# Two blocks of the shared up projection ahead of the last tiles' transposition, and the shared down weights in quarters

## The chip, the cores and the metric

The kernel runs on one core of one Trainium2 chip. The metric is the device time of one execution in microseconds (us). The kernel before took 1296.97 us, the median of three runs (1294.72, 1296.97 and 1297.15). A core has five engines that run side by side, each with its own instruction order: TensorE (PE), VectorE (DVE), ScalarE (ACT), GpSimd (POOL) and SyncE (SP, which here only issues transfers). They wait for each other by semaphores.

## The reference, cut to what matters

One transformer block on x of 2 x 1024 tokens with 512 features: attention, then a mixture of experts.

```
x = x + attention(layernorm(x))          # 32 heads, 8 key heads, causal
n = layernorm(x).reshape(2048, 512)
logits = n @ router_w                    # 64 experts
scores = softmax(logits);  idx = top_k(logits + router_bias, 4)
gate   = scores[idx] / sum(scores[idx])
routed = sum over the 4 experts of gate * (silu(n @ wg[e]) * (n @ wu[e])) @ wd[e]
shared = sum over s = 0, 1 of (silu(n @ swg[s]) * (n @ swu[s])) @ swd[s]      # swg: 512 x 512
out = x + routed + shared
```

## The kernel before, in words

Tokens lie in 16 tiles of 128 (`t`), and four tiles make a group (`g`) of 512 tokens. The order of every engine is written out by hand; nothing is scheduled by a planner. After attention comes the part that the change touches:

1. **Output projection and second layer norm.** PE projects a group of four tiles (`project`, L1056). DVE adds the result to `X` (L1372), takes the statistics (L1375, L1379) and writes the normalised rows `xn2` (L1389). PE then transposes them (`turn_tokens`, L1065), ACT copies the transposed tile twice (L811 in fp32, L812 in f16 for `x_hi`), PE multiplies with the router (`logits`, L1073), and DVE forms `x_lo`, what the f16 copy lacks (L1362). PE's order is project group 0, project group 1, turn and logits of group 0, project group 2, turn and logits of group 1, and so on; turn and logits of group 3 (tiles 12 to 15) come last.
2. **Routing, on DVE.** It starts only when the logits of all 16 tiles are there (`logits_done`): maximum (L1415), subtraction (L1416), top eight and their indices (L1419, L1422, L1424), then per chosen expert a one-hot matrix (L1427), its product with the exponentials `ex` (L1429) and a sum (L1430), then sums over the tiles (L1438, L1439). That raises `masks_ready`. PE then runs `ranks` (L1093 to L1096), one more block of the shared projection, and `starts` (L1102); DVE goes on with these to slot numbers (L1450 to L1481), and last to the one-hot matrices of the slot table (L1499, L1502), with additions of the shared result in between (L1495).
3. **The shared experts.** A group of 512 tokens has eight up blocks (`n` or `hc` = 0 to 7), each of 24 matmuls in f16: 2 weights (gate and up) x 4 slices x 3 parts (hi x hi, hi x lo, lo x hi; L1130). ACT takes silu (L829) and copies the up half (L833), POOL multiplies them (`hidden`, L706, raises `hidden_done`), ACT rounds that to f16 (`hidden_high`, L821) and POOL forms the rest (`hidden_low`, L698). Block `n` of PE waits for `hidden_done` of block `n - 2`. After the eight blocks come four down tiles (L1151). `ranks` stands behind block 5, `starts` behind block 6. In the second group the product is DVE's (L1485), so PE's block 10 waits for DVE to be done with its table matrices.
4. **The shared down weights `swd`.** Two transfers of 1 MB each bring them to `w_stage`; POOL scales each half (L689), ACT rounds it to f16 (L815, `swd_high` in the new code), POOL forms what is left (L693). All of that stands ahead of `hidden` in POOL's order and ahead of `ex` and silu in ACT's order. PE and SP wait for it with `swd_lo_ready`.

After this region come 96 pairs of 64-slot tiles for the routed experts, the shared experts for groups 2 and 3, and the output.

Of the kernel before, what the change touches and what calls it, by code (L numbers as in the profile page):

```python
# [8 lines left out]
ACT = mybir.ActivationFunctionType  # L9
ALU = mybir.AluOpType  # L10
AXX = mybir.AxisListType.X

P = 128
BATCH, SEQ, D = 2, 1024, 512
NTOK = BATCH * SEQ
NT = NTOK // P
C = D // P
# [3 lines left out]
BANK = 512  # L21
E, F, TOPK = 64, 128, 4
HID = 1024
HC = HID // P
# [10 lines left out]


EARLY = 2

TABLE_AT = HC + 4

# [9 lines left out]
X_SCALE, W_SCALE = 16.0, 64.0  # L50
# [104 lines left out]
def build_block(nc, x, wq, wk, wv, wo, router_w, router_bias, wg, wu, wd, swg, swu, swd, out):  # L155
    ctx = ExitStack()
    with ctx:
# [72 lines left out]
        def q_part(u, h, part):  # L230
# [11 lines left out]
        x_hi, x_lo = carve_all(flat_xn, 0, *[([P, C, NTOK], F16)] * 2)  # L242
        w_stage, x_turned = carve_all(ring, 0, ([P, 2, C * D], FP32), ([P, 4, C * P], FP32))
# [3 lines left out]
        shared_w, swd_w, tmp, mask, cum = carve_all(  # L247
            att, 0, ([P, 4, 2 * C * D], F16), ([P, 2, HC * D], F16), ([P, NT, E], FP32),
            ([P, NT, E], BF16), ([P, NT, E], BF16))
        shared_w = shared_w.rearrange("p n (s d) -> p n s d", s=2 * C)  # L250
        swd_w = swd_w.rearrange("p n (s d) -> p n s d", s=HC)
# [32 lines left out]
        def bank(k, n=BANK):  # L284
            return PS[:, k * BANK:k * BANK + n]
# [49 lines left out]
        swd_scaled = sem("swd_scaled")  # L335
        swd_hi_ready = sem("swd_hi_ready")
        swd_lo_ready = sem("swd_lo_ready")
        hidden_hi_done = sem("hidden_hi_done")
        hidden_lo_done = sem("hidden_lo_done")
        x1_done = sem("x1_done")  # L340
# [10 lines left out]
        x_lo_ready = sem("x_lo_ready")  # L351
        w_hi_ready = sem("w_hi_ready")
        w_lo_ready = sem("w_lo_ready")
        stage_in = [sem("stage_in0"), sem("stage_in1")]
        logits_done = sem("logits_done")
        consts = sem("consts")
        route = sem("route")
        ex_ready = sem("ex_ready")
# [11 lines left out]
        up_done = sem("up_done")  # L370
        silu_done = sem("silu_done")
        up_copied = sem("up_copied")
        hidden_done = sem("hidden_done")
# [61 lines left out]
        def _(sp):  # L435
# [4 lines left out]
            for r in range(REP):  # L440
                for k in range(2):
                    at = (2 * r + k) * HD
# [118 lines left out]
                load_down(i, JP - 1, codes[JP - 1])  # L561

            sp.wait_ge(experts_in, 16)
            sp.wait_ge(swd_lo_ready, 2)
            sp.wait_ge(table_done, 1)
            load_pairs(0, True)
            with sp.Fori(1, LANE_TILES) as i:
# [9 lines left out]
        def _(pool):  # L577
# [106 lines left out]
            pool.affine_select(out=tile_no[:, LANES:], in_=tile_no[:, LANES:], compare_op=ALU.is_gt, fill=-1.0, base=0,  # L684
                               pattern=[[0, LANES]], channel_multiplier=1).then_inc(consts, 1)

            for k in range(2):
                pool.wait_ge(stage_in[k], 16 * 3)
                pool.tensor_scalar(w_stage[:, k, :], w_stage[:, k, :], W_SCALE, None, ALU.mult).then_inc(swd_scaled, 1)  # L689
            for k in range(2):  # L690
                pool.wait_ge(swd_hi_ready, k + 1)
                part = slice(k * C, (k + 1) * C)
                pool.tensor_tensor(swd_w[:, 1, part, :], w_stage[:, k, :].rearrange("p (c n) -> p c n", c=C),  # L693
                                   swd_w[:, 0, part, :], ALU.subtract).then_inc(swd_lo_ready, 1)

            def hidden_low(n):
                pool.wait_ge(hidden_hi_done, n + 1)
                pool.tensor_tensor(hidden_lo[:, n, :], hidden(n), hidden_hi[:, n, :], ALU.subtract)\  # L698
                    .then_inc(hidden_lo_done, 1)

            for n in range(HC):
                pool.wait_ge(silu_done, n + 1)
                pool.wait_ge(up_copied, n + 1)
                if n >= 2:
                    pool.wait_ge(hidden_lo_done, n - 1)
                pool.tensor_tensor(hidden(n), silu_s[:, n % 2, :], up_s[:, n % 2, :], ALU.mult)\  # L706
                    .then_inc(hidden_done, 1)
                if n:
                    hidden_low(n - 1)
            hidden_low(HC - 1)  # L710

            for k in range(TOPK):
# [34 lines left out]
        def _(act):  # L747
# [48 lines left out]
            for g in range(4):  # L796
# [7 lines left out]
                for t in range(4 * g, 4 * g + 4):  # L804
# [5 lines left out]
                    src = bank(4 + t % 2).rearrange("p (c t) -> p c t", c=C)  # L810
                    act.activation(x_turned[:, t % 4, :, :], src, ACT.Copy).then_inc(xt2_ready, 1)  # L811
                    act.activation(x_hi[:, :, t * P:(t + 1) * P], src, ACT.Copy, scale=X_SCALE).then_inc(x_hi_ready, 1)  # L812
            for k in range(2):
                act.wait_ge(swd_scaled, k + 1)
                act.activation(swd_w[:, 0, k * C:(k + 1) * C, :], w_stage[:, k, :].rearrange("p (c n) -> p c n", c=C),  # L815
                               ACT.Copy).then_inc(swd_hi_ready, 1)
            act.wait_ge(route, 2)
            act.activation(ex[:, :, :], tmp[:, :, :], ACT.Exp).then_inc(ex_ready, 1)
            def hidden_high(n):
                act.wait_ge(hidden_done, n + 1)  # L820
                act.activation(hidden_hi[:, n % HC, :], hidden(n), ACT.Copy).then_inc(hidden_hi_done, 1)  # L821

            def shared_silu(g):
                for n in range(HC * g, HC * (g + 1)):
                    act.wait_ge(up_done, n + 1)

                    if n >= 2:
                        act.wait_ge(hidden_done, n - 1)
                    act.activation(silu_s[:, n % 2, :], bank(2 * (n % 2)), ACT.Silu,  # L829
                                   scale=1 / (X_SCALE * W_SCALE)).then_inc(silu_done, 1)  # L830
                    if g == 0:

                        act.activation(up_s[:, n % 2, :], bank(2 * (n % 2) + 1), ACT.Copy,  # L833
                                       scale=1 / W_SCALE).then_inc(up_copied, 1)
                    if n > HC * g:
                        hidden_high(n - 1)
                hidden_high(HC * (g + 1) - 1)

            for g in range(EARLY):
# [45 lines left out]
        def _(pe):  # L885
# [158 lines left out]
            def project(t):  # L1044

                pe.wait_ge(yt_done, C * (t // QT + 1))
                if t == 0:

                    pe.wait_ge(wo_in, 16 * 8)
                    pe.wait_ge(router_in, 16)  # L1050
                    pe.wait_ge(exp_done, 2 * NS * BATCH * KVH)
                    pe.wait_ge(side_read, SIDE * BATCH * KVH)
                if t >= 4:
                    pe.wait_ge(x1_done, t - 3)
                for c in range(C):
                    mm = pe.matmul(bank(t % 4), YT[:, c, t * P:(t + 1) * P], wo_s[:, c, :],  # L1056
                                   start=(c == 0), stop=(c == C - 1))
                mm.then_inc(wo_done, 1)
# [10 lines left out]
            def logits(t):  # L1069
# [4 lines left out]
                                   start=(c == 0), stop=(c == C - 1))  # L1074
                mm.then_inc(logits_done, 1)

            for g in range(5):
                if g < 4:
                    for t in range(4 * g, 4 * g + 4):
                        project(t)  # L1080
                if g >= 1:
                    for t in range(4 * g - 4, 4 * g):
                        turn_tokens(t)
                    for t in range(4 * g - 4, 4 * g):
                        logits(t)
# [28 lines left out]
                                           start=(k == 0 and t == 0), stop=(k == TOPK - 1 and t == NT - 1))  # L1114
                mm.then_inc(table_done, 1)

            pe.wait_ge(x1_done, NT)
            pe.wait_ge(w_lo_ready, 4)
            def shared(g):
                pe.wait_ge(x_lo_ready, 4 * (g + 1))  # L1120
                for hc in range(HC):
                    n = HC * g + hc
                    if n >= 2:
                        pe.wait_ge(hidden_done, n - 1)
                    s, at = hc // C, (hc % C) * P
                    tokens = slice(g * BANK, (g + 1) * BANK)
                    for k in range(2):
                        for c in range(C):
                            for w, v in ((0, x_hi), (0, x_lo), (1, x_hi)):
                                mm = pe.matmul(bank(2 * (n % 2) + k), shared_w[:, 2 * k + w, C * s + c, at:at + P],  # L1130
                                               v[:, c, tokens], start=(c == 0 and w == 0 and v is x_hi),
                                               stop=(c == C - 1 and w == 1))
                    mm.then_inc(up_done, 1)
                    if g == 0 and hc == RANKS_AT:
                        ranks()
                    if g == 0 and hc == STARTS_AT:
                        starts()
                    if n == TABLE_AT:
                        table()
                if g == 0:  # L1140

                    pe.wait_ge(experts_ready, 1)
                    pe.wait_ge(swd_lo_ready, 2)
                for t in range(4 * g, 4 * g + 4):
                    if t >= 2:
                        pe.wait_ge(shared_added, t - 1)
                    for hc in range(HC):
                        if t == 4 * g:
                            pe.wait_ge(hidden_lo_done, HC * g + hc + 1)
                        for w, v in ((0, hidden_hi), (0, hidden_lo), (1, hidden_hi)):  # L1150
                            mm = pe.matmul(bank(4 + t % 2), v[:, hc, (t % 4) * P:(t % 4 + 1) * P], swd_w[:, w, hc, :],  # L1151
                                           start=(hc == 0 and w == 0 and v is hidden_hi),
                                           stop=(hc == HC - 1 and w == 1))
                    mm.then_inc(down_done, 1)
# [469 lines left out]
```

## Time and profile before

| | before |
|---|---|
| median of 3 runs | 1296.97 us |
| lowest to highest | 1294.72 to 1297.15 us |
| the profiled execution's own time | 1296.95 us |
| its span | 1294.9 us |
| mean granted TensorE clock | 0.976 |
| PE / DVE / ACT / POOL busy | 91 / 58 / 38 / 27% of the span |

The span is the time between the first and the last event of the profiled execution; some 2 us lie around it. Shares of busy time are averages over stages that have different limits, so the stretch that the change touches, from about 600 to 760 us, has to be read by itself. A timeline row gives the start, the time covered, the engine and line, the operation, the tile written and the tile read, the partitions x elements and how many instructions were merged, and in brackets the idle time before it and who ended it.

### The profile page before, as it was taken

How to read it: one execution, taken by the hardware profiler on the slowest of the kernel's cores; microseconds unless marked ns; L12 is line 12 of the kernel's file. 1: busy time of each engine (PE TensorE's matmuls, PEld its weight loads, DVE VectorE, ACT ScalarE, POOL GpSimd, SP SyncE). 2: the span in 40 equal slices, each digit the busy share in tenths (PEclk: the TensorE clock that was granted, in tenths of full speed). 3: DMA queues.
4: the chain of work that ended last, by engine and by line, in shares of the span. 5: the costliest groups of instructions: out<-in, count | busy, mean ns of one | idle time of the engine just before them, and what ended most of it. 6: DMA issues, size and time to landing. Idle time of an engine off the chain costs nothing.

```text
span 1294.9 us, 27720 instructions
## 1 busy us (share of the span) xinstructions
PE 1173.3 (91%) x8853; PEld 538.6 (42%) x8854; DVE 745.4 (58%) x1215; ACT 489.9 (38%) x922; POOL 348.9 (27%) x458
## 2 busy tenths in 40 slices
PE   6989788988998998999789989999999999999898
PEld 3534233333333332356333445555444444543343
DVE  5335798999899995557987212233232322327374
ACT  2111587887788788334320212222222221211010
POOL 1000122222222222101736112322222322217561
PEclk9989799999999999999898999999999999999899
DMA  7333232132132120233000347887887688837552
GB/s 228 101 82 102 41 75 39 38 69 41 37 61 49 37 56 2 83 112 131 1 1 1 115 141 251 257 259 261 274 266 244 199 305 311 260 96 230 164 157 70
DMA packets 85556, 169.96 MB, mean 131 GB/s; under 512 B 14852, under 2 KB 17412, under 8 KB 85508
## 3 DMA queue, kind: packets, MB, share of 16 engines
q1 hardware_dynamic: 55764, 100.60, 26.2%
q0 software_dynamic: 12800, 41.95, 11.6%
q10 hardware_dynamic: 16944, 26.75, 6.0%
q8 instruction: 32, 0.52, 0.2%
q14 instruction: 16, 0.13, 0.0%
HBM read 225.08 MB, written 41.42 MB: 206 GB/s over the span
## 4 chain that ended last, share of the span: by engine, by line
PE 53%; DVE 18%; issue 9%; DMA 8%; SPq 5%; POOL 3%; ACT 2%; DVEq 0%; ACTq 0%; POOLq 0%
PE PS L1178 9%; PE PS L1130 6%; DVE maxes L1250 6%; PE PS L957 6%; PE PS L1004 5%; PE PS L1151 5%; PE PS L1194 5%; DVE max_low L1252 5%; PE PS L1056 4%; PE PS L894 4%; DMA ring<-in_L_ffn_wu_dram 3%; PE PS L1165 3%; POOL ring L742 3%; SPq L540 2%; PE PS L982 2%
## 5 line engine op out<-in xcount | busy, mean ns | idle before, releaser
L788 ACT ACTIVATE att<-PS 128x512 f32<-128x512 f32 x576 | 312.4, 595 | 95.0 <-PE PS L982 89.5
L1250 DVE TENSOR_REDUCE maxes<-PS 128x2 f32<-128x128 f32 (+7 forms) x256 | 186.8, 749 | 35.3 <-PE PS L899 34.9
L1130 PE MATMUL PS<-XN,att 128*128 128x512 f16 x768 | 172.9, 387 | 15.5 <-POOL w_att L706 7.9
L1004 PE MATMUL PS<-att,v_head 128*32 128x256 f32 (+1 forms) x2560 | 181.7, 375 | 0.9 <-POOL att L635 0.9
L894 PE MATMUL PS<-att 48*128 48x512 f16 (+7 forms) x768 | 128.3, 332 | 50.1 <-DVE max_low L1252 24.3
L1252 DVE TENSOR_REDUCE max_low<-PS 128x2 f32<-128x1024 f32 x128 | 154.9, 1210 | 12.7 <-PE PS L894 12.5
L1536 DVE TENSOR_TENSOR w_att<-w_att,PS 128x128 f32<-128x128 f32 x96 | 27.6, 288 | 203.9 <-ACT w_att L851 203.9
L846 ACT ACTIVATE w_att<-PS 128x512 f32<-128x512 f32 x96 | 57.2, 597 | 171.8 <-PE PS L1165 169.9
L1130 PEld LDWEIGHTS PS<-XN,att 128*128 128x128 f16 x768 | 75.4, 99 | 111.3 <-POOL w_att L706 8.4
L635 POOL TENSOR_SCALAR_AFFINE_SELECT att<-att 128x512 f32<-128x512 f32 (+1 forms) x96 | 74.9, 787 | 165.4 <-ACT att L788 164.2
L982 PE MATMUL PS<-att 50*128 50x512 f16 (+1 forms) x640 | 112.9, 365 | 4.8 <-ACT att L788 2.6
L894 PEld LDWEIGHTS PS<-att 48*128 48x128 f16 x768 | 37.3, 93 | 192.0 <-DVE maxes L1250 81.5
L724 POOL DMA_INDIRECT w_att<-xn_rows,idx x96 | 93.5, 974 | 75.6 <-POOL idx L722 74.8
L1548 DVE COPY w_att<-PS 128x512 f32<-128x512 f32 x96 | 66.4, 692 | 74.9 <-DMA slot_y<-w_att 47.0
L1178 PE MATMUL PS<-ring,w_att 128*64 128x256 f32 x768 | 95.6, 390 | 11.4 <-DMA ring<-in_L_ffn_wu_dram 10.1
L1178 PE MATMUL PS<-XT,w_att 128*64 128x256 f32 x768 | 93.4, 385 | 8.9 <-issue 4.6
L1151 PE MATMUL PS<-att,XT 128*128 128x512 f16 x384 | 87.3, 388 | 9.0 <-DVE XT L1490 6.6
L829 ACT ACTIVATE w_att<-PS 128x512 f32<-128x512 f32 x32 | 19.1, 597 | 188.4 <-PE PS L1130 188.4
L742 POOL DMA_INDIRECT ring<-slot_y,small x64 | 69.5, 1086 | 67.7 <-DMA slot_y<-w_att 29.3
L1004 PEld LDWEIGHTS PS<-att,v_head 128*32 128x32 f32 x2560 | 56.8, 110 | 71.7 <-issue 46.0
L1165 PEld LDWEIGHTS PS<-ident,w_att 128*128 128x128 f32 x384 | 53.6, 209 | 75.2 <-issue 75.0
L851 ACT ACTIVATE w_att<-PS 128x128 f32<-128x128 f32 x96 | 26.6, 277 | 150.6 <-PE PS L1178 150.6
(167 smaller groups left out, 1337.6 us busy)
## 6 DMA issues: line engine op xcount, KB each, us to landing
ring<-in_L_ffn_wg_dram SPq DMA_DIRECT2D x96, 256.0 KB
ring<-in_L_ffn_wu_dram SPq DMA_DIRECT2D x96, 256.0 KB
ring<-in_L_ffn_wd_dram SPq DMA_DIRECT2D x96, 256.0 KB
XT<-in_L_ffn_wg_dram SPq DMA_DIRECT2D x96, 256.0 KB
XT<-in_L_ffn_wu_dram SPq DMA_DIRECT2D x96, 256.0 KB
XT<-in_L_ffn_wd_dram SPq DMA_DIRECT2D x96, 256.0 KB
slot_y<-w_att ACTq DMA_DIRECT2D x192, 128.0 KB
att<-q_stacks SPq DMA_DIRECT2D x64, 192.0 KB, 3.9
```

Source lines behind the costliest of these rows:

```text
L724: pool.indirect_dma_start(out=xg[:, j, :], out_offset=None, in_=xn2_rows[:, :], in_offset=bass.IndirectOffsetOnAxis(ap=idx[:, j:j + 1], ax ...
L742: pool.indirect_dma_start(out=yk[:, t % YK, k, :], out_offset=None, in_=slot_y[:, :], in_offset=bass.IndirectOffsetOnAxis(ap=slot_u[:, k, ...
L788: act.activation(probs[:, n0 % RING, u * BANK:(u + 1) * BANK], bank((2 * n0 + u) % EXP_BANKS), ACT.Exp, scale=HD ** -0.5 / QK_SCALE ** 2). ...
L894: mm = pe.matmul(bank(at + u, n), q_max[b][rows, t * P:(t + 1) * P], k_max[b][rows, lo:lo + n], start=True, stop=not diagonal)
L982: mm = pe.matmul(PS[:, at:at + 2 * qn], k_exp[b][rows, kt * P:(kt + 1) * P], q_exp[b][rows, 2 * q0:2 * (q0 + qn)] .rearrange("p (t h q) -> ...
L1004: mm = pe.matmul(PS[32 * r:32 * r + 32, at:at + qn], v_head[b][:, kt, :], probs[:, (NS * b + s) % RING, a:a + qn], start=s in (0, NS0), st ...
L1130: mm = pe.matmul(bank(2 * (n % 2) + k), shared_w[:, 2 * k + w, C * s + c, at:at + P], v[:, c, tokens], start=(c == 0 and w == 0 and v is x ...
L1151: mm = pe.matmul(bank(4 + t % 2), v[:, hc, (t % 4) * P:(t % 4 + 1) * P], swd_w[:, w, hc, :], start=(hc == 0 and w == 0 and v is hidden_hi) ...
L1165: mm = pe.transpose(PS[:, (k % 2) * BANK + c * P:(k % 2) * BANK + (c + 1) * P], xg[:, j, c:D:C], ident[:, :])
L1178: mm = pe.matmul(PS[l * SUB:(l + 1) * SUB, at:at + 2 * F], xgt[:, j % 2, c * P + l * SUB:c * P + (l + 1) * SUB], lane_w[2 * j + l][:, 0:2, ...
L1250: dve.reduce_max(maxes[b][:, :, t], src, AXX).then_inc(side_read, 1)
L1252: dve.reduce_max(max_low[:, :, t - LOW_TILES], src, AXX).then_inc(side_read, 1)
```

## The change: what it does

- PE: two up blocks of group 0 (`AHEAD_UP = 2`, blocks 0 and 1) are issued ahead of `turn_tokens` and `logits` of tiles 12 to 15. They wait for `x1_done` of all tiles, `w_lo_ready` 3 and `x_lo_ready` 4. The remaining blocks stand where they stood.
- POOL and ACT: the shared down weights are handled in quarters of 1024 elements per partition. POOL scales two quarters ahead of the blocks and two in blocks 1 and 2, and forms the low parts in blocks 3 to 6; ACT rounds quarters 0 and 1 in block 2, 2 in block 4 and 3 in block 5. ACT's `ex` moves behind the silu of block 1. The semaphores count to 4 in place of 2.

```
@@ SP, and PE ahead of the down tiles
-            sp.wait_ge(swd_lo_ready, 2)
+            sp.wait_ge(swd_lo_ready, 4)
@@ POOL
-            for k in range(2):
-                pool.wait_ge(stage_in[k], 16 * 3)
-                pool.tensor_scalar(w_stage[:, k, :], ...).then_inc(swd_scaled, 1)
-            for k in range(2):
-                pool.wait_ge(swd_hi_ready, k + 1)
-                pool.tensor_tensor(swd_w[:, 1, part, :], ..., ALU.subtract).then_inc(swd_lo_ready, 1)
+            swd_scale(0)
+            swd_scale(1)
             for n in range(HC):
                 ... hidden(n), hidden_low(n - 1)
+                if n in (1, 2):
+                    swd_scale(n + 1)
+                if n in (3, 4, 5, 6):
+                    swd_low(n - 3)
@@ ACT
-            for k in range(2):
-                act.wait_ge(swd_scaled, k + 1)
-                act.activation(swd_w[:, 0, k * C:(k + 1) * C, :], ...).then_inc(swd_hi_ready, 1)
-            act.wait_ge(route, 2)
-            act.activation(ex[:, :, :], tmp[:, :, :], ACT.Exp).then_inc(ex_ready, 1)
             ... silu and copy of block n
+                    if n == AHEAD_UP - 1:
+                        act.wait_ge(route, 2)
+                        act.activation(ex[:, :, :], tmp[:, :, :], ACT.Exp).then_inc(ex_ready, 1)
                     if n > HC * g:
                         hidden_high(n - 1)
+                    for half in {2: (0, 1), 4: (2,), 5: (3,)}.get(n, ()):
+                        swd_high(half)
@@ PE
             for g in range(5):
                 if g < 4:
                     ... project(t)
+                if g == 4:
+                    pe.wait_ge(x1_done, NT)
+                    pe.wait_ge(w_lo_ready, 3)
+                    pe.wait_ge(x_lo_ready, 4)
+                    for hc in range(AHEAD_UP):
+                        shared_up(0, hc)
                 if g >= 1:
                     ... turn_tokens(t), then logits(t)
```

PE's order at the end of the layer norm stage, before. The rows with `ident,w_att` are the transpositions of tiles 12 to 15 (the last of them here), those with `router_s` the logits, those with `XN,att` the up blocks:

```order
L1065 MATMUL PS<-ident,w_att 128x128 [waits x_hi_ready,xn2_ready]
L1065 MATMUL PS<-ident,w_att 128x128 x3
L1073 MATMUL PS<-router_s,ring 128x64 [waits xt2_ready]
L1073 MATMUL PS<-router_s,ring 128x64 x3
L1130 MATMUL PS<-XN,att 128x512 [waits x_lo_ready,w_lo_ready,x1_done]
L1130 MATMUL PS<-XN,att 128x512 x47
L1130 MATMUL PS<-XN,att 128x512 [waits hidden_done]
```

The same place in the changed kernel, from the logits of tile 11 on:

```order
L1092 MATMUL PS<-router_s,ring 128x64 x3
L1105 MATMUL PS<-XN,att 128x512 [waits x_lo_ready,w_lo_ready,x1_done]
L1105 MATMUL PS<-XN,att 128x512 x47
L1084 MATMUL PS<-ident,w_att 128x128 [waits x_hi_ready,xn2_ready]
L1084 MATMUL PS<-ident,w_att 128x128 x3
```

The 48 matmuls of blocks 0 and 1 moved from behind the logits of tiles 12 to 15 to ahead of their transpositions.

POOL's order before, from the scaling of the down weights (`ring<-ring`) over their low parts (`att<-ring,att`) to the first `hidden` (`w_att<-w_att`) and `hidden_low` (`XT<-w_att,XT`):

```order
L689 TENSOR_SCALAR ring<-ring 128x2048 [waits stage_in0]
L689 TENSOR_SCALAR ring<-ring 128x2048 [waits stage_in1]
L693 TENSOR_TENSOR att<-ring,att 128x2048 [waits swd_hi_ready] x2
L706 TENSOR_TENSOR w_att<-w_att 128x512 [waits up_copied,silu_done] x2
L698 TENSOR_TENSOR XT<-w_att,XT 128x512 [waits hidden_hi_done]
```

The same stretch in the changed kernel, to block 3:

```order
L695 TENSOR_SCALAR ring<-ring 128x1024 [waits stage_in0] x2
L715 TENSOR_TENSOR w_att<-w_att 128x512 [waits up_copied,silu_done] x2
L705 TENSOR_TENSOR XT<-w_att,XT 128x512 [waits hidden_hi_done]
L695 TENSOR_SCALAR ring<-ring 128x1024 [waits stage_in1]
L715 TENSOR_TENSOR w_att<-w_att 128x512 [waits hidden_lo_done,up_copied,silu_done]
L705 TENSOR_TENSOR XT<-w_att,XT 128x512 [waits hidden_hi_done]
L695 TENSOR_SCALAR ring<-ring 128x1024 [waits stage_in1]
L715 TENSOR_TENSOR w_att<-w_att 128x512 [waits hidden_lo_done,up_copied,silu_done]
L705 TENSOR_TENSOR XT<-w_att,XT 128x512 [waits hidden_hi_done]
L700 TENSOR_TENSOR att<-ring,att 128x1024 [waits swd_hi_ready]
```

The first `hidden` no longer stands behind the two low parts, and each quarter now stands between the small steps of a block.

ACT's order before, from the rounding of the down weights (`att<-ring`) over `ex` (`XT<-att`) to silu and copy (`w_att<-PS`):

```order
L815 ACTIVATE att<-ring 128x2048 [waits swd_scaled] x2
L818 ACT_TABLE_LOAD
L818 ACTIVATE XT<-att 128x1024 [waits route]
L829 ACT_TABLE_LOAD
L829 ACTIVATE w_att<-PS 128x512 [waits up_done]
```

And in the changed kernel:

```order
L843 ACT_TABLE_LOAD
L843 ACTIVATE w_att<-PS 128x512 [waits up_done]
L847 ACTIVATE w_att<-PS 128x512
L843 ACTIVATE w_att<-PS 128x512 [waits up_done]
L847 ACTIVATE w_att<-PS 128x512
L851 ACT_TABLE_LOAD
L851 ACTIVATE XT<-att 128x1024 [waits route]
L835 ACTIVATE XT<-w_att 128x512 [waits hidden_done]
L843 ACT_TABLE_LOAD [waits hidden_done]
L843 ACTIVATE w_att<-PS 128x512 [waits up_done]
```

Silu and copy of blocks 0 and 1 now stand first, and there is one table load more.

## Rows read from the trace of the kernel before

**Rows 1.** The chain of waits, 609 to 630 us: start, us, what.

```profile
609.59 4.97 DMA ring<-in_L_ffn_swd_dram
614.63 5.37 POOL ring L689
...
624.41 4.75 DVE XT L1427
```

**Rows 2.** The timeline of PE, 604 to 723 us.

```profile
604.79 1.04 PE L1065 MATMUL PS<-ident,w_att 128*128 128x128 f32 x8
...
608.34 3.68 PE L1073 MATMUL PS<-router_s,ring 128*128 128x64 f32 x32
611.86 10.52 PE L1130 MATMUL PS<-XN,att 128*128 128x512 f16 x48
630.32 22.86 PE L1130 MATMUL PS<-XN,att 128*128 128x512 f16 x96 [7.93 <-POOL w_att L706]
654.74 0.38 PE L1094 MATMUL PS<-att,small 128*128 128x512 bf16 x1 [1.57 <-DVEq L1440]
...
655.61 5.35 PE L1130 MATMUL PS<-XN,att 128*128 128x512 f16 x24
660.89 0.20 PE L1102 MATMUL PS<-small 64*128 64x64 bf16 x1
...
679.45 10.53 PE L1151 MATMUL PS<-att,XT 128*128 128x512 f16 x48 [0.94 <-DVE X L1495]
...
703.38 18.68 PE L1130 MATMUL PS<-XN,att 128*128 128x512 f16 x72 [3.04 <-DVE w_att L1485]
```

**Rows 3.** The timeline of DVE, 603 to 703 us.

```profile
603.04 1.92 DVE L1389 TENSOR_SCALAR w_att<-X,mv,rstd 128x512 f32<-128x512 f32 x4
...
612.12 1.23 DVE L1415 TENSOR_REDUCE small<-PS 128x16 f32<-128x1024 f32 x1
...
621.30 2.83 DVE L1424 CAST small<-small 128x128 f32<-128x128 uint32 x1
...
643.37 1.23 DVE L1427 TENSOR_TENSOR XT<-small 128x1024 bf16<-128x1024 f32 x1
...
654.21 0.20 DVE L1439 TENSOR_TENSOR small<-att 128x64 bf16<-128x64 bf16 x1
...
661.13 0.22 DVE L1457 COPY small<-PS 128x64 f32<-128x64 f32 x1 [2.59 <-PE PS L1102]
```

**Rows 4.** DVE's groups by line, 621.28 to 654.45 us: busy us, mean ns | idle before.

```profile
L1427 DVE TENSOR_TENSOR XT<-small 128x1024 bf16<-128x1024 f32 x4 | 9.2, 2303 | 0.4 <-ACT XT L818 0.3
L1429 DVE TENSOR_TENSOR att<-XT 128x1024 f32<-128x1024 bf16 x4 | 7.7, 1932 | 0.1
L1430 DVE TENSOR_REDUCE small<-att 128x16 f32<-128x1024 f32 x4 | 4.9, 1220 | 0.1
L1438 DVE TENSOR_TENSOR att<-att 128x64 bf16<-128x64 bf16 x15 | 4.7, 315 | 0.5
...
L1434 DVE TENSOR_TENSOR att<-att,XT 128x1024 bf16<-128x1024 bf16 x2 | 1.4, 692 | 0.1
```

**Rows 5.** The timeline of POOL, 614 to 657 us.

```profile
614.63 5.36 POOL L689 TENSOR_SCALAR ring<-ring 128x2048 f32<-128x2048 f32 x1 [15.02 <-DMA ring<-in_L_ffn_swd_dram]
619.97 8.09 POOL L693 TENSOR_TENSOR att<-ring,att 128x2048 f16<-128x2048 f32 x2
...
650.49 1.15 POOL L698 TENSOR_TENSOR XT<-w_att,XT 128x512 f16<-128x512 f32 x1
```

**Rows 6.** Stretches: us, then busy of PE, PEld, DVE, ACT, POOL, PEclk, DMA share, GB/s.

```profile
630.00:634.00 4.00, 3.68 (x9) 1.33 (x10) 3.93 (x3) 0.63 (x1) 3.58 (x3) 0.50 0.02 4
634.00:638.00 4.00, 4.00 (x19) 1.81 (x18) 3.86 (x5) 0.33 (x1) 0.00 (x0) 0.96 0.00 0
```

**Rows 7.** The timeline of ACT, 609 to 626 us.

```profile
609.03 0.66 ACT L812 ACTIVATE XN<-PS 128x512 f16<-128x512 f32 x1
...
624.32 1.28 ACT L829 ACT_TABLE_LOAD   x1
```

More of the change, by code:

```diff
@@ L37 @@
 EARLY = 2
+AHEAD_UP = 2
 TABLE_AT = HC + 4
@@ L685, in _, with swd_half, swd_scale, swd_low @@
                                pattern=[[0, LANES]], channel_multiplier=1).then_inc(consts, 1)
-            for k in range(2):
-                pool.wait_ge(stage_in[k], 16 * 3)
-                pool.tensor_scalar(w_stage[:, k, :], w_stage[:, k, :], W_SCALE, None, ALU.mult).then_inc(swd_scaled, 1)
-            for k in range(2):
-                pool.wait_ge(swd_hi_ready, k + 1)
-                part = slice(k * C, (k + 1) * C)
-                pool.tensor_tensor(swd_w[:, 1, part, :], w_stage[:, k, :].rearrange("p (c n) -> p c n", c=C),
-                                   swd_w[:, 0, part, :], ALU.subtract).then_inc(swd_lo_ready, 1)
+            def swd_half(n):
+                part = slice(n % 2 * C // 2, (n % 2 + 1) * C // 2)
+                return w_stage[:, n // 2, :].rearrange("p (c n) -> p c n", c=C)[:, part, :]
+            def swd_scale(n):
+                pool.wait_ge(stage_in[n // 2], 16 * 3)
+                pool.tensor_scalar(swd_half(n), swd_half(n), W_SCALE, None, ALU.mult).then_inc(swd_scaled, 1)
+            def swd_low(n):
+                pool.wait_ge(swd_hi_ready, n + 1)
+                part = slice(n * C // 2, (n + 1) * C // 2)
+                pool.tensor_tensor(swd_w[:, 1, part, :], swd_half(n), swd_w[:, 0, part, :], ALU.subtract)\
+                    .then_inc(swd_lo_ready, 1)
             def hidden_low(n):
@@ L812, in _, with swd_high @@
                     act.activation(x_hi[:, :, t * P:(t + 1) * P], src, ACT.Copy, scale=X_SCALE).then_inc(x_hi_ready, 1)
-            for k in range(2):
-                act.wait_ge(swd_scaled, k + 1)
-                act.activation(swd_w[:, 0, k * C:(k + 1) * C, :], w_stage[:, k, :].rearrange("p (c n) -> p c n", c=C),
-                               ACT.Copy).then_inc(swd_hi_ready, 1)
-            act.wait_ge(route, 2)
-            act.activation(ex[:, :, :], tmp[:, :, :], ACT.Exp).then_inc(ex_ready, 1)
+            def swd_high(n):
+                act.wait_ge(swd_scaled, n + 1)
+                part = slice(n % 2 * C // 2, (n % 2 + 1) * C // 2)
+                act.activation(swd_w[:, 0, n * C // 2:(n + 1) * C // 2, :],
+                               w_stage[:, n // 2, :].rearrange("p (c n) -> p c n", c=C)[:, part, :], ACT.Copy)\
+                   .then_inc(swd_hi_ready, 1)
             def hidden_high(n):
@@ L1075, in logits, with shared_up @@
                 mm.then_inc(logits_done, 1)
+            def shared_up(g, hc):
+                n = HC * g + hc
+                if n >= 2:
+                    pe.wait_ge(hidden_done, n - 1)
+                s, at = hc // C, (hc % C) * P
+                tokens = slice(g * BANK, (g + 1) * BANK)
+                for k in range(2):
+                    for c in range(C):
+                        for w, v in ((0, x_hi), (0, x_lo), (1, x_hi)):
+                            mm = pe.matmul(bank(2 * (n % 2) + k), shared_w[:, 2 * k + w, C * s + c, at:at + P],
+                                           v[:, c, tokens], start=(c == 0 and w == 0 and v is x_hi),
+                                           stop=(c == C - 1 and w == 1))
+                mm.then_inc(up_done, 1)
             for g in range(5):
@@ L1115, in table @@
                 mm.then_inc(table_done, 1)
-            pe.wait_ge(x1_done, NT)
-            pe.wait_ge(w_lo_ready, 4)
             def shared(g):
+                pe.wait_ge(w_lo_ready, 4)
                 pe.wait_ge(x_lo_ready, 4 * (g + 1))
@@ L1122, in shared @@
                     n = HC * g + hc
[L1123 to L1133, printed above, removed]
+                    if n >= AHEAD_UP:
+                        shared_up(g, hc)
                     if g == 0 and hc == RANKS_AT:
@@ L1142, in shared @@
                     pe.wait_ge(experts_ready, 1)
-                    pe.wait_ge(swd_lo_ready, 2)
+                    pe.wait_ge(swd_lo_ready, 4)
                 for t in range(4 * g, 4 * g + 4):
```

## The prediction, as it was put on record

> **What bounds the kernel now.** I read the page first: PE is busy 91% of the span, but that is an average, so it says little about the 150 us the change touches. Then PE's timeline of that stretch, looking for idle time [rows 2]. The largest hole is 7.93 us ahead of the third up block, put down to POOL's `hidden`. Before it PE ran without a gap worth naming, from the projections through the turn and logits of tiles 12 to 15 (604.79 to 612.0) and blocks 0 and 1 (611.86 to 622.38). After it PE stands three more times, each time for DVE: 1.57 us ahead of `ranks`, 0.94 us in the down tiles, 3.04 us ahead of block 10. So even with the 7.93 us hole in front, PE catches up with DVE at `ranks` and has to wait. Whatever PE gains before 654.74 us ends in that wait, unless DVE is earlier too.
>
> Third, the chain of waits [rows 1]. It runs over the second transfer of the down weights, POOL's scaling and ACT's `ex` into DVE's first one-hot product at 624.41. That looks as if the down weights set the time. But DVE's timeline [rows 3, 4] shows that its own work was as late: the cast in front of that product ended at 621.30 + 2.83 = 624.13, and DVE then waited only 0.28 us for `ex`. DVE's work goes back to L1415 at 612.12, which began as the last logits ended: 608.34 + 3.68 = 612.02. From there DVE works to 703 us with one wait that counts, 2.59 us for `starts`. So there are two nearly equal chains into 624.4 and one out of it: the logits of tile 15, 91 us of DVE, then PE's block 10 at 703.38 and all that follows.
>
> **PE's order.** The change puts 48 matmuls ahead of the turn of tile 12. Was PE waiting there? No: `xn2` of tiles 12 to 15 was written from 603.04 to 604.96 [rows 3], its first tile after some 0.5 us, and PE came to it at 604.79 [rows 2], straight from the logits of tile 11, with no wait. The blocks' own operands are there too, so they start at 604.79. Their price: row 611.86 covers 10.52 us for 48; the last one covers 0.38 us and the pace is 0.216 us, so the next work starts 10.52 - 0.38 + 0.22 = 10.4 us later. Turn, logits and L1415 all move by that: **+10.4 us**, L1415 at 622.5. DVE meanwhile has nothing to fill the gap with.
>
> **What PE gets back, and where it ends.** ACT's copies of the last tiles end at 609.69 + 10.4 = 620.1 [rows 7]. Silu of block 0 follows: a table load of 1.28 us, then silu and the copy, some 1.1 together at the pace of L812 (0.66 alone, overlapped), so 622.5; POOL's `hidden` takes 1.15, as the same-sized L698 does [rows 5]. Block 2 starts near 623.7 with PE free at 622.4: the hole of 7.93 us shrinks to about 1.3, and blocks 2 to 5 could be done by 623.7 + 4 x 5.2 = 644.5, a few us later if POOL lags. `ranks` needs DVE, which is not before 660. The hole reappears there, 14 to 18 us long. Worth of the gain: 0.
>
> **DVE up to `masks_ready`.** From L1415 to the cast DVE took 9.2 us beside POOL without being slowed. From the cast to the end of L1439 it took 654.41 - 621.30 = 33.1 us. A clean L1427 took 1.23 [rows 3]; I take the same for L1429, and the reduction L1430 took 1.22 every time. Clean: 12 x 1.22 = 14.7; three mask sums of 0.69; fifteen L1438 at 0.20 + 0.03, 3.5; cast, memset and L1439 0.5; gaps 0.5: 21.3 us. So 33.1 - 21.3 = 11.8 us were stalls, all in operations with two SBUF inputs and in the cast, while POOL was in tensor-tensor operations; L1430 was never stretched [rows 4]. POOL's work in that stretch: the rest of the first L693, 2.7, the second, 4.05, and five `hidden` and four `hidden_low` of 1.15, 10.4, which makes 17.1 us: 0.69 us of stall per us of POOL. After the change there stand in the same stretch three low quarters of 2.02 (half of 4.05), 6.1, four `hidden` and four `hidden_low`, 9.2, and one scaling quarter of 2.68. Whether scaling holds DVE up the trace doesn't show, as L689 ran beside nothing of that kind. Without it 15.3 x 0.69 = 10.5, with it 18.0 x 0.69 = 12.4 us of stall. Against 11.8 that is -1.3 to +0.6. The last POOL steps may come behind DVE's chain, so I take a little under the middle: **-0.7**. `ex` needs only L1416, so it is ready near 627.5 and DVE needs it at 632: no wait, even with the added table load. The low end of the range needs more: if short quarters slip beside L1430 and stalls halve, -6.
>
> The Trainium skill ("SBUF — State Buffer", section "SBUF: two separate sides") says that the port pair shared by VectorE and GpSimd is an exclusive lock, held for a whole instruction, by whichever starts first of a GpSimd operation and a VectorE operation with two SBUF inputs or in a two-port mode. The stretches of L1427 and of the cast agree. By the page scaling holds the lock as well, which takes the upper figure, +0.6 in place of -0.7, and the forecast 1.3 us higher.
>
> **PE behind its new wait.** `ranks`, block 6 and `starts` are on the path: in the trace block 6 ran 655.61 to 660.9 and DVE waited 2.59 us for `starts` [rows 2, 3]. After the 7.93 us hole PE ran at a granted clock of 0.50, 1.2 GHz, from 630 to 634 [rows 6]: 96 matmuls took 22.86 us where 96 x 0.216 = 20.7 would do, 2.1 lost. After the 3.04 us hole 72 took 18.68 against 15.6, 3.1 lost. The new hole is longer than either, so PE comes to `ranks` and block 6 at the low clock: between 2.1 and 3.1, **+2.5**. Before, the loss of 2.1 lay ahead of a wait and cost nothing; now it lies on the path. The loss at block 10 stays.
>
> **The last low quarter.** It stands in block 6, behind `hidden_low` of block 5, and must be done before PE's down tiles. That is 2.02 us of POOL between `hidden` 6 and 7, which had a pause of that size; it may stall DVE or PE for 0 to 2 us. DVE needs the down tiles only at 678.7. Take **+0.3**.
>
> **Sum.** 10.4 - 0.7 + 2.5 + 0.3 = +12.5 us at block 10, which starts at 716. Behind 703.38 nothing changes its order, and PE runs without a break into the routed experts, so the shift stays. The execution's own 1296.95 + 12.5 = 1309.5 us; the median of before is 1296.97, the same within the spread. SP's two changed waits are met long before `table_done`, which moves with the rest.
>
> **Rivals.**
> - *Light loss.* DVE regains half of its stalls since no POOL operation is longer than 2.7 us: 10.4 - 6 + 2.1 = +6.5, 1303.4. For: the longest stalls were the cast and the first L1427, 2.6 and 3.5 us beside L693. Against: four quarters hold as much as two halves, and POOL and DVE took turns in the trace.
> - *Heavy loss.* Scaling blocks too, the low clock costs 3.1 us and the last quarter 2: 10.4 + 0.6 + 3.1 + 2 = +16.1, 1313.
> - *Faster: the hole of 7.93 us was the bound.* If DVE's chain had slack, PE would gain 7.93 - 1.3 and the low clock behind the hole, 2.1: -8.7, 1288.2. It decides if DVE's chain has more than 10.4 us of slack at `ranks`. For: it is PE's longest wait here, and the chain of waits goes over the down weights. Against: PE waited 1.57 us for DVE at `ranks` with the hole in front.
> - *No change:* the delay of the logits is met exactly by what DVE gains. That takes 10.4 + 2.5 of stalls, and there are 11.8; next to excluded.
>
> **How the numbers follow.** Forecast 0.70, light 0.15, heavy 0.08, faster 0.05, no change 0.02. The forecast's own range is 1306.5 to 1312; with most of the light and heavy cases, 1303 to 1314. A measurement of this kernel tells 0.2%, 2.6 us, from no change. Slower by over 0.2%: 0.70 + 0.15 + 0.08 = 0.93; within 0.02; faster 0.05.
>
> **What the profile after would show.** PE's 48 up matmuls from 604.8, and L1415 at 622.5 (right: the push is whole). A wait of at most 2 us ahead of block 2 (right: the hole is gone). An idle time of 14 to 18 us ahead of `ranks`, ended by DVE, and L1439 ending near 664 (right: DVE's chain is the bound). A granted clock of 0.50 in `ranks` and the first half of block 6. Block 10 with its two followers starting near 716. If L1415 starts near 612 still, or if PE doesn't wait at `ranks`, the forecast is wrong at its root; if L1439 ends below 660, the light case holds.

## The result: slower, and the profile after

The changed kernel took 1311.22 us, the median of four runs (1307.59 to 1315.82), against 1297.06 us for the kernel before beside it. The ratio is 1.0107, with a 95% interval of 1.0065 to 1.0149. Two more comparisons, made with the experiments, gave 1.0078 (1.0051 to 1.0105) and 1.0051 (1.0019 to 1.0083). All three say slower, by 7 to 14 us; the forecast was 12.5. The profiled execution took 1311.55 us, with a span of 1309.5 us against 1294.9.

PE's timeline after, in the columns of [rows 2]:

```profile
524.73 27.73 PE L1075 MATMUL PS<-w_att,XT 128*128 128x512 f32 x64
...
600.37 10.52 PE L1105 MATMUL PS<-XN,att 128*128 128x512 f16 x48
610.73 1.04 PE L1084 MATMUL PS<-ident,w_att 128*128 128x128 f32 x8
...
614.04 3.68 PE L1092 MATMUL PS<-router_s,ring 128*128 128x64 f32 x32
619.35 20.88 PE L1105 MATMUL PS<-XN,att 128*128 128x512 f16 x96 [1.63 <-POOL w_att L715]
656.54 0.61 PE L1133 MATMUL PS<-att,small 128*128 128x512 bf16 x1 [16.31 <-DVEq L1470]
...
658.50 7.30 PE L1105 MATMUL PS<-XN,att 128*128 128x512 f16 x24
665.74 0.20 PE L1142 MATMUL PS<-small 64*128 64x64 bf16 x1
...
686.08 12.22 PE L1181 MATMUL PS<-att,XT 128*128 128x512 f16 x48 [3.04 <-DVE X L1525]
...
711.14 15.71 PE L1105 MATMUL PS<-XN,att 128*128 128x512 f16 x72 [2.47 <-DVE w_att L1515]
```

Set beside [rows 2], the hole of 7.93 us ahead of block 2 has shrunk to 1.63, and the 1.57 us of waiting at `ranks` have become 16.31, ended by DVE. What PE gained it gave back at the next point where it meets DVE. `ranks` and block 6, 0.87 and 5.28 us from start to start before, took 1.96 and 7.24. (One row is missing in [rows 2]: of the four large matmuls of `ranks` this profile of the kernel before holds only the last three. Its second profile has all four, and there `ranks` takes 1.09 us, from 653.30 to 654.39. So 0.87 stands for 1.09 us, and the wait ahead of it was 1.35 us and not 1.57.)

The absolute times hide something: in this execution attention ended earlier, so the first projection began at 524.73 where it began at 529.15 before. From here on times are counted from that row, and the **stage** is the time from it to the start of block 10 (the x72 row): 703.38 - 529.15 = 174.2 us before, 711.14 - 524.73 = 186.4 us after, 12.2 more. It is the same in every profile of a kernel to within about 1 us, which the total is not.

DVE's timeline after answers to [rows 3]:

```profile
617.82 1.23 DVE L1445 TENSOR_REDUCE small<-PS 128x16 f32<-128x1024 f32 x1 [1.70 <-PE PS L1092]
...
627.00 0.32 DVE L1454 CAST small<-small 128x128 f32<-128x128 uint32 x1
...
656.23 0.19 DVE L1469 TENSOR_TENSOR small<-att 128x64 bf16<-128x64 bf16 x1
...
665.98 0.23 DVE L1487 COPY small<-PS 128x64 f32<-128x64 f32 x1 [6.38 <-PE PS L1142]
...
669.75 2.05 DVE L1495 TENSOR_SCALAR small<-small 24x8 f32<-24x8 f32 x1
```

The routing starts 93.1 us after the first projection, against 83.0: the delay of the two blocks. From the cast to L1469 it needed 29.4 us against 33.1. The groups by line of that stretch, 626.98 to 656.45 us, stand beside [rows 4]:

```profile
L1459 DVE TENSOR_TENSOR att<-XT 128x1024 f32<-128x1024 bf16 x4 | 8.1, 2030 | 0.1
L1457 DVE TENSOR_TENSOR XT<-small 128x1024 bf16<-128x1024 f32 x4 | 8.1, 2025 | 0.1
L1460 DVE TENSOR_REDUCE small<-att 128x16 f32<-128x1024 f32 x4 | 4.9, 1220 | 0.1
L1468 DVE TENSOR_TENSOR att<-att 128x64 bf16<-128x64 bf16 x15 | 2.9, 192 | 0.5
```

The one very long product is gone, but now the products of both kinds take 2.0 us on average (1.7 to 2.2) where a clean one takes 1.2, and POOL works without a pause beside them, from 621.99 to 652.11 us. The fifteen small sums are clean (192 ns against 315), as POOL waits for block 6 by then.

### The profile page after: what moved, and what is told of

It is laid out like the page before. It is cut to its first block, busy times and chain, and to the rows that moved or that the text cites. A ratio compares the mean times of both kernels' runs of the same rounds, so it can differ in the third digit from the quotient of the medians.

```text
span 1309.5 us, 27730 instructions
## 1 busy us (share of the span) xinstructions
PE 1172.1 (90%) x8854; PEld 536.3 (41%) x8854; DVE 741.3 (57%) x1215; ACT 491.1 (38%) x925; POOL 353.7 (27%) x462
## 4 chain that ended last, share of the span: by engine, by line
PE 56%; DVE 19%; issue 9%; DMA 6%; SPq 6%; ACT 2%; another core or an unknown queue 1%; POOL 1%; DVEq 0%; ACTq 0%; POOLq 0%
PE PS L1208 10%; PE PS L1105 8%; DVE maxes L1280 6%; PE PS L976 6%; PE PS L1023 5%; PE PS L1181 5%; PE PS L1224 5%; DVE max_low L1282 4%; PE PS L1075 4%; PE PS L913 3%; PE PS L1195 3%; SPq L542 2%; PE PS L1001 2%; DMA ring<-in_L_ffn_wu_dram 2%; SPq L536 2%
## 5 line engine op out<-in xcount | busy, mean ns | idle before, releaser
L1280 DVE TENSOR_REDUCE maxes<-PS 128x2 f32<-128x128 f32 (+7 forms) x256 | 186.8, 749 | 33.9 <-PE PS L918 33.5
L1566 DVE TENSOR_TENSOR w_att<-w_att,PS 128x128 f32<-128x128 f32 x96 | 27.7, 288 | 209.8 <-issue 124.8
L1023 PEld LDWEIGHTS PS<-att,v_head 128*32 128x32 f32 x2560 | 56.5, 109 | 71.5 <-issue 45.3
```

The source lines that it names most:

```text
L1023: mm = pe.matmul(PS[32 * r:32 * r + 32, at:at + qn], v_head[b][:, kt, :], probs[:, (NS * b + s) % RING, a:a + qn], start=s in (0, NS0), st ...
L1280: dve.reduce_max(maxes[b][:, :, t], src, AXX).then_inc(side_read, 1)
```

## The experiments

The table holds the parts of the stage in us: from the first projection to the start of the routing (L1415 in the kernel before), from the cast to the end of L1439, from the first row of `ranks` to `starts` on PE, from DVE's first step behind `starts` (L1457) to the first shared addition (L1495), and from there to block 10. Line numbers differ between the kernels, and the parts are the same. The 9.2 us from L1415 to the cast, the same in all, and some 0.3 us between the engines are left out. The first matmul of `ranks` has no row in the first and third profile before and in the third after: 6.2 is 6.4 there, and 8.9 is about 9.3.

| kernel | routing starts | cast to masks | ranks to starts | starts to addition | addition to block 10 | stage |
|---|---|---|---|---|---|---|
| before (3 profiles) | 83.0 | 33.1, 33.0, 33.9 | 6.2, 6.4, 6.2 | 17.6 | 24.7 | 174.2, 174.2, 175.1 |
| after (3 profiles) | 93.1 | 29.4, 29.4, 30.4 | 9.2, 9.2, 8.9 | 19.4 | 25.8 | 186.4, 186.4, 187.4 |
| order only | 93.1 | 27.8 | 8.2 | 17.6 | 24.7 | 180.9 |
| quarters only | 83.0 | 34.1 | 8.7 | 19.4 | 25.7 | 180.4 |
| one block ahead | 87.9 | 31.5 | 8.2 | 19.4 | 25.4 | 182.0 |
| after, wait filled | 93.1 | 29.5 | 6.4 | 19.4 | 25.7 | 183.5 |
| low parts and ranks | 83.0 | 27.7 | 3.8 | 20.4 | 24.7 | 169.0 |
| low parts placed | 83.0 | 27.7 | 8.8 | 17.6 | 24.7 | 171.2 |

**Order only.** PE as in the changed kernel, POOL and ACT as before.

```
+                if g == 4:
+                    pe.wait_ge(x1_done, NT); pe.wait_ge(w_lo_ready, 3); pe.wait_ge(x_lo_ready, 4)
+                    for hc in range(2): shared_up(0, hc)
                 if g >= 1: ... turn_tokens, logits
```

> Only PE's order is changed: blocks 0 and 1 ahead of the turn of tiles 12 to 15; the down weights stay in halves, ex stays ahead of silu. The stage is measured from the first projection (L1056, x64) to block 10 (the up group x72): 174.2 us before, 186.4 after the whole change. Theory A (the delayed logits are the cost: L1415 10.1 us later against the stage's start): stage 181 to 185, since the two low parts of POOL now run ahead of DVE's cast and no longer stall it. Rival B (the quarters cost the time, by stalling DVE and stretching ranks): stage near 174 and the time near that of before. Rival C (the hole of 7.93 us ahead of block 2 is the bound): the hole stays at some 8 us here, because hidden still stands behind the low parts, so the time is unchanged or longer.

Measured: ratio 1.0033 (1.0002 to 1.0064), stage 180.9, +6.6. Theory A's range held; rival B fell, as the order alone costs more than half of the loss. The routing starts 10.1 us later, and 5.3 us of that come back, because POOL's low parts now run while DVE takes its maximum and top eight. Another 1.9 us go from `ranks` to `starts` (8.2 against 6.4), behind a wait of 4.92 us. POOL's timeline in this kernel:

```profile
618.47 8.09 POOL L695 TENSOR_TENSOR att<-ring,att 128x2048 f16<-128x2048 f32 x2 [1.61 <-ACT att L817]
626.52 2.49 POOL L708 TENSOR_TENSOR w_att<-w_att 128x512 f32<-128x512 f32 x2
```

and DVE's:

```profile
628.21 0.89 DVE L1437 CAST small<-small 128x128 f32<-128x128 uint32 x1
629.13 2.07 DVE L1440 TENSOR_TENSOR XT<-small 128x1024 bf16<-128x1024 f32 x1
```

(L1437 is the cast, L1440 the first product.) Both low parts end at 626.56, ahead of the cast at 628.21; before, the second ended at 628.06 and the cast wanted to start at 621.30. The hole ahead of block 2 was 9.00 us here, longer than the 7.93 before: it belongs to the place of the low parts ahead of `hidden`, as rival C says, but quarters only, the next experiment, shows that it is not what sets the time.

**Quarters only.** PE as before; POOL and ACT as in the changed kernel, with `ex` ahead of silu.

```
-                if g == 4: ... shared_up(0, 0), shared_up(0, 1)
-AHEAD_UP = 2
+AHEAD_UP = 0
```

> Only the down weights are handled in quarters; PE's order is that of before (turn and logits of tiles 12 to 15, then blocks 0 and 1), and ex stands ahead of silu. Theory A: L1415 starts 83 us after the first projection, as before; the hole ahead of block 2 is gone, but DVE's chain from the cast to L1439 takes 29 to 30 us (33.1 before), PE waits some 10 us at ranks and comes to it at the low clock (3 us lost there), the last quarter stalls DVE by up to 1.9 us: stage 173 to 177 (174.2 before), time within 4 us of before. Rival C (the hole of 7.93 us was the bound): stage 165 to 168, time 6 to 9 us below before.

Measured: ratio 1.0035 (1.0007 to 1.0064), stage 180.4, +6.1. Rival C is refuted: the hole ahead of block 2 was gone altogether, and the stage did not become shorter. But theory A was wrong here, by 3.4 us at the upper end of its range: I had carried over the 29 to 30 us from the cast to the masks, and it was 34.1. With the logits early, all of POOL's scaling and low quarters fall on DVE's chain, the fifteen small sums included:

```profile
642.14 8.72 DVE L1461 TENSOR_TENSOR att<-att 128x64 bf16<-128x64 bf16 x15
```

and POOL's steps that they met:

```profile
641.36 2.57 POOL L700 TENSOR_TENSOR att<-ring,att 128x1024 f16<-128x1024 f32 x1
643.89 1.25 POOL L715 TENSOR_TENSOR w_att<-w_att 128x512 f32<-128x512 f32 x1
645.11 1.15 POOL L705 TENSOR_TENSOR XT<-w_att,XT 128x512 f16<-128x512 f32 x1
646.22 2.11 POOL L700 TENSOR_TENSOR att<-ring,att 128x1024 f16<-128x1024 f32 x1
```

Clean, those sums take 3.35 us, as in the changed kernel; here 5.4 more. Against the kernel before, though, that stretch is only 1.0 us longer (34.1 against 33.1). The rest of the 6.1 lies behind it: 2.3 us from `ranks` to `starts`, behind a wait of 12.35 us, 1.8 up to the first addition, beside the last low quarter, and 1.0 up to block 10. So the quarters cost by themselves, and the two parts nearly add: 6.6 + 6.1 = 12.7 against 12.2 together.

**One block ahead.** `AHEAD_UP = 1` in the changed kernel.

> The changed kernel with one block ahead of the last tiles in place of two; ex then follows silu of block 0. Theory A (each block ahead delays the logits by its own 5.2 us): L1415 at 88.1 us after the first projection (83.0 with none, 93.1 with two), and the stage to block 10 between that of the quarters alone (180.4) and of the whole change (186.4): 181 to 185 us. Rival B (the place of the blocks does not matter, the quarters do): L1415 at 93 or stage at 186 still.

Measured: ratio 1.0054 (1.0028 to 1.0080), stage 182.0, inside theory A's range. The routing starts at 83.0, 87.9 and 93.1 us with no, one and two blocks ahead, close to the price of a block each time. The stage does not move in step (180.4, 182.0, 186.4), since the later DVE starts, the fewer of POOL's steps it meets: 34.1, 31.5 and 29.4 us to the masks.

**The wait filled.** The changed kernel with more work.

```
             def ranks():
+                for _ in range(66):
+                    pe.matmul(bank(5), shared_w[:, 0, 0, 0:P], x_hi[:, 0, 0:BANK], start=True, stop=True)
                 pe.wait_ge(masks_ready, 1)
```

> The changed kernel with 66 matmuls added whose result nobody reads (128x512 f16 into a free bank), put between block 5 and ranks, where PE otherwise waits 16.3 us for DVE. They should fill 14.3 us of that wait. Theory A (the low clock behind the wait costs 3 us on the path): ranks takes 0.9 us in place of 1.96 and block 6 takes 5.3 in place of 7.3, DVE gets starts 3 us earlier, stage 182 to 184 us in place of 186.4, although PE has 14 us more work. Rival E (the slow ranks and block 6 are something else, or other work hides them): stage 186 or longer.

Measured: stage 183.5, 2.9 us shorter with 14.4 us of matmuls more. PE's timeline in it:

```profile
639.88 14.41 PE L1130 MATMUL PS<-XN,att 128*128 128x512 f16 x66
656.38 0.39 PE L1135 MATMUL PS<-att,small 128*128 128x512 bf16 x1 [2.09 <-DVEq L1472]
...
657.47 5.35 PE L1105 MATMUL PS<-XN,att 128*128 128x512 f16 x24
```

`ranks` is back at 1.09 us and block 6 at 5.29, and the granted clock was 1.00 from 656 to 664 us. In the changed kernel the granted clock after the 16.31 us of idling stood at its lower level, 0.50 (1.2 GHz), all through 654 to 662 us:

```profile
654.00:662.00 8.00, 5.46 (x14) 1.83 (x15) 3.90 (x20) 0.00 (x0) 0.00 (x0) 0.50 0.00 0
662.00:664.00 2.00, 2.00 (x10) 0.86 (x9) 0.00 (x0) 0.00 (x0) 0.00 (x0) 0.88 0.03 8
...
712.00:716.00 4.00, 4.00 (x20) 1.86 (x19) 0.79 (x1) 0.00 (x0) 0.24 (x1) 1.00 0.00 0
```

(Columns as in [rows 6]; the last row lies in block 10.) The stage was at the upper end of what I expected, and rival E fell. The whole ratio, 1.0076 (1.0044 to 1.0108), does not show the gain: it lies inside the scatter of the rest.

**Before and after again.** Unchanged kernels, for the scatter between executions.

> The kernel before, profiled again, to see what its own stages do from one execution to the next. Theory A (what lies outside the stage is noise): the attention part up to the first projection (529.2 us in the first profile), the routed part (first expert tile to the end, 533.8 us) each move by some us between two profiles of the same kernel; the stage to block 10 stays within 1 us of 174.2. Rival D (the change itself lengthens the routed part, 543.6 us in the first profile after): before stays at 534 within 2 us.

> The changed kernel again, timed against before in five more rounds. Theory A: stage within 1 us of 186.4, block 10 at the full clock again, time +9 to +15 us against before; the routed part anywhere from 533 to 544 us. Rival D (the change lengthens the routed part): it takes 543 us again, and shows the same 15.9 us pause of ACT near 1191 us.

> The kernel before, a third profile. So far the part up to the first projection took 529.1 and 528.0 us in it, and 523.2 to 525.9 us in eight profiles of kernels whose instructions up to there are the same. If that is scatter between executions, this one may fall anywhere from 523 to 529; if the kernel before is bound to it, 528 to 529. Stage to block 10: 174.2, the part behind the stage anywhere.

> The changed kernel, a third profile beside the third of before. Stage to block 10 at 186.4 and to the first expert tile at 241.2 us once more. Routed part: 396.6 in both profiles so far, 393.1 and 393.4 in before; if that belongs to the change it is 396 to 397 again, if it is scatter it may be 392 to 397.

Measured, in us, with the time from block 10 to the first expert tile, from there to the shared group 2, and from there to the end:

| profile | to the first projection | stage | to first expert tile | routed tiles | the rest | span |
|---|---|---|---|---|---|---|
| before | 529.1 | 174.2 | 57.7 | 393.1 | 140.7 | 1294.9 |
| before, 2nd | 528.0 | 174.2 | 56.5 | 393.4 | 147.6 | 1299.6 |
| before, 3rd | 527.2 | 175.1 | 56.4 | 397.9 | 139.4 | 1296.0 |
| after | 524.7 | 186.4 | 54.8 | 396.6 | 147.0 | 1309.5 |
| after, 2nd | 524.3 | 186.4 | 54.8 | 396.6 | 143.9 | 1306.0 |
| after, 3rd | 525.5 | 187.4 | 54.8 | 392.9 | 140.5 | 1301.0 |

The ratios of the unchanged kernel were 0.9997 and 0.9999. Rival D is refuted: the routed tiles took 393 to 398 us in both kernels, and with the rest it is 534 to 541 us before and 533 to 544 after. The rest scatters by 8.2 us before and 6.5 after. The first two profiles after had long pauses of ACT in it, of 15.89 and 14.43 us, and the second before had a like one of 13.08 us.

**Low parts and ranks, and low parts placed.** From what the first two experiments showed: leave the logits early, and put POOL's long steps where DVE has no operation that they stall.

```
 POOL
+            swd_scale(0); swd_scale(1); swd_low(0); swd_low(1); swd_scale(2); swd_scale(3)
             for n in range(HC): ... hidden(n), hidden_low(n - 1)
+                if n == RANKS_AT:
+                    pool.wait_ge(masks_ready, 1)
+                    swd_low(2); swd_low(3)
 ACT: rounds quarters 0 and 1 ahead of ex, 2 and 3 in block 2
 PE: AHEAD_UP = 0, and in the first of the two
-RANKS_AT = 5
-STARTS_AT = 6
+RANKS_AT = 6
+STARTS_AT = 7        # in the middle of block 7, between its gate and its up half
```

> An attempt at a version that beats both. PE's order of before (logits first). The down weights in quarters, but placed where DVE needs no second SBUF input: POOL forms low quarters 0 and 1 while DVE takes maximum and top eight, quarters 2 and 3 when masks_ready is up, during DVE's short steps and its wait for starts. ranks stands behind block 6 in place of 5, and starts in the middle of block 7 in place of behind block 6. Theory A (DVE's chain from the logits is the bound): L1439 ends at 119 to 122 us after the first projection (125.3 before), DVE's wait for starts falls below 1.5 us, stage 165 to 170 us in place of 174.2, time 4 to 9 us below before. Rival F (POOL's small steps stall DVE as much as the low parts did): L1439 at 124 or later, stage 171 to 175.

> As e7, but ranks and starts stay behind blocks 5 and 6. It tells the gain of the placed low parts from that of ranks and starts. Theory A: L1439 as in e7, 119 to 122 us; PE waits some 8 us at ranks and comes to it at the low clock, so DVE's wait for starts is 5 to 6 us: stage 170 to 174 us, time 0 to 4 us below before. Rival F: stage 174 or longer.

Measured: with both, ratio 0.9971 (0.9946 to 0.9996), stage 169.0, -5.2; with the low parts alone 0.9974 (0.9947 to 1.0001), stage 171.2, -3.0. The masks were up at 119.8 us in both, against 125.3 before, as theory A expects; rival F fell. In the first PE no longer stands at `ranks`:

```profile
618.64 26.07 PE L1111 MATMUL PS<-XN,att 128*128 128x512 f16 x120 [0.42 <-POOL w_att L719]
644.91 0.39 PE L1134 MATMUL PS<-att,small 128*128 128x512 bf16 x1 [0.19 <-DVEq L1470]
...
646.00 2.76 PE L1111 MATMUL PS<-XN,att 128*128 128x512 f16 x12
648.70 0.20 PE L1143 MATMUL PS<-small 64*128 64x64 bf16 x1
```

In the second it waits 5.36 us and pays 8.8 us from `ranks` to `starts`. Of the 5.0 us between the two there, 2.8 go again: in the first POOL's low quarters 2 and 3 fall on DVE's steps behind `starts` (20.4 against 17.6), in the second into the 3.12 us in which DVE waits for `starts`. The first version is faster than the kernel before by 0.3%, 3.7 us by the ratio, just under the 4 to 9 expected; for the second the interval just includes no change.

## Why the prediction was right, point by point

- **DVE's chain from the last logits is the bound: right.** PE waited 16.31 us at `ranks` (forecast 14 to 18), for DVE. Quarters only closed the hole ahead of block 2 and was not faster.
- **The push, +10.4: right.** L1415's counterpart started 10.1 us later, and 4.9 us with one block. The other 0.2 came back inside the transpositions, where PE waited 0.83 us for ACT and not 1.06.
- **The stalls up to the masks, -0.7: too small.** It was 33.1 to 29.4, -3.7, about halfway to the low end of -6: 8.1 us of stalls in place of 11.8. The prediction gave an end of L1439 below 660 as the sign of the light case. Its counterpart ended at 656.42, and at 660.8 with the 4.4 us by which this execution reached the first projection earlier: in this term the kernel stood between forecast and light case. The ratio of stall to POOL's time was carried over from a stretch with two 4 us steps. With steps of 2 us and less, part of them lies beside the reduction L1430's counterpart, and the last had ended before the small sums began.
- **The low clock, +2.5: 2.8 measured** (0.9 in `ranks`, counted from the 1.09 us of four matmuls, and 2.0 in block 6), and the same 2.8 came back between `ranks` and `starts` when the wait was filled.
- **The last low quarter, +0.3: mis-sized.** The part from `starts` to the addition grew by 1.8 us: L1495 took 2.05 us beside the quarter at 669.66. And a step was missing: DVE's additions fell behind, PE waited 3.04 us in the down tiles instead of 0.94 and worked on at a clock of 0.83 on average (680 to 690 us), which cost 1.1 us more.
- **The sum, +12.5 at block 10: 12.2**, since 10.1 - 3.7 + 2.8 + 1.8 + 1.1 = 12.1, the rest being rounding. That it came so close is in part luck: one term was 3.0 us too high, and against it stood 1.5 and 0.3 us too low and 1.1 that was missing.
- **"The loss at block 10 stays": wrong.** PE waited 2.47 us there and not 3.04, the clock stayed at 1.00 (row 712 to 716 above), and the 72 matmuls took 15.71 us, not 18.68 (17.40 in the other two profiles before). Up to the first expert tile that gave back 2.9 us against the first profile before, and 2.1 against the mean of three.
- **The rest.** By the means of three profiles the span grew by 8.7 us: 12.3 from the stage, -2.1 behind it, -3.3 from attention, and +1.8 from the routed tiles and the end, which is scatter. The profile of the first comparison had one of the long ends. The three ratios give 13.9, 10.1 and 6.6 us, with intervals of 0.3 to 0.4% to each side and not the 0.2% that the prediction counted on. So the forecast of the mechanism holds by the stage, and the total change is nearer to 9 or 10 us than to 12.5.

**Open.** Attention took 527.2 to 529.1 us in three profiles of the kernel before and 523.2 to 525.9 in all nine profiles of the other kernels, which differ from it only behind attention. The instructions there are the same, and no experiment was made on it. What pauses ACT and PE near 1190 us in some executions was not found either.

## What to carry to other kernels

A hole in the busiest engine is worth only as much as the next meeting point leaves: look where that engine waits next, for whom, and what starts that one's chain; work put ahead of that start costs its full length. Splitting a helper's steps did not by itself make its neighbour faster here (34.1 us against 33.1 to the masks, with the logits at their old place); placing them where DVE has no operation that collides did (27.7 us). And an idle stretch moved onto the path brings the matmuls behind it at the lower clock as well; here 14 us of matmuls whose result nobody reads made the stage 2.9 us shorter.

## What the runs showed of the hardware

- POOL's scaling (one input) and its tensor-tensor operations stall DVE differently. In quarters only, a scaling quarter waited for DVE's running product, then both overlapped:

```profile
621.04 2.04 DVE L1450 TENSOR_TENSOR XT<-small 128x1024 bf16<-128x1024 f32 x1
623.11 1.94 DVE L1452 TENSOR_TENSOR att<-XT 128x1024 f32<-128x1024 bf16 x1
```

```profile
621.96 3.74 POOL L695 TENSOR_SCALAR ring<-ring 128x1024 f32<-128x1024 f32 x1
```

  A clean quarter takes 2.7 us, so by POOL's rows it ran from about 623.0 to 625.7. The product at 623.11 ended at 625.05, before the quarter did, and lost 0.7 us, not 2.6. The section of the Trainium skill that the prediction weighs ("SBUF — State Buffer", "SBUF: two separate sides") would have the product wait to the end; for this pair the measurement says otherwise. For POOL's tensor-tensor operations the trace agrees with it: in the kernel before the first product, begun at 624.41, ended at 629.16, 1.1 us behind the end of the second low part at 628.06, and a clean one takes 1.2.
- A small DVE operation with one input suffers as well: L1495 on 24 x 8 elements took 2.05 us beside a low quarter, and 0.16 in the kernel before.
- A wait of 2.47 us left the clock at its upper level in all six profiles that had it (15.71 us for the 72 matmuls); waits of 3.04 us ahead of block 10 were followed by the lower level in five profiles (17.09 to 18.68 us for the 72 matmuls) and not in one (15.71 in the kernel with the low parts placed).
